# A state-space scan layer with one activation table set in its front, and in its loop a quarter of d*u spread by DMA and multiplied on GpSimd

## The reference, cut to what matters

```
d   = softplus(W_k xc + bias_k)                      # 96 channels
dA  = exp(d * A[k, c, s])
h_t = h_(t-1) * dA_t + (d_t * u_t) * B_t[s]
y_t = sum over s of h_t[s] * C_t[s]                  # and + Dsk * u
```

## Time and profile before

| | us |
|---|---|
| median of 3 runs | 1020.37 |
| lowest, highest | 1018.37, 1024.68 |
| the profiled execution's own time | 1026.5 |
| its span, first to last instruction | 1024.7 |

### The profile page before, as it was taken

The page is one execution under the profiler, slowest core; times in us unless marked ns, Lnnn a source line. Parts: engine busy times, 40 slices in busy tenths (PEclk is TensorE's granted clock), DMA queues, the critical chain, the costliest instruction groups (busy, mean ns, idle before and its releaser), DMA issues. The chain is left out here.

```text
span 1024.7 us, 17912 instructions
## 1 busy us (share of the span) xinstructions
PE 889.6 (87%) x6186; PEld 592.7 (58%) x6186; DVE 748.7 (73%) x1612; ACT 572.8 (56%) x1007; POOL 486.8 (48%) x502
## 2 busy tenths in 40 slices
PE   8769999997699987879988679999999987766985
PEld 3323333334258972234445359899888845566985
DVE  6479999998476537877875776788888685583665
ACT  2765455431246645978963645777776265264762
POOL 0006666663206632799882005377777400034873
PEclk8889999999799987555556979999999987978997
DMA  5067666631300009300000192999995573203464
GB/s 141 1 175 189 156 168 169 167 104 28 65 1 1 2 13 267 3 1 2 1 2 1 47 233 77 260 264 266 258 266 149 159 223 106 62 24 104 167 211 163
DMA packets 73018, 120.19 MB, mean 117 GB/s; under 512 B 24704, under 2 KB 47632, under 8 KB 72928
## 3 DMA queue, kind: packets, MB, share of 16 engines
q1 hardware_dynamic: 68080, 108.85, 40.1%
q0 software_dynamic: 4848, 10.20, 2.9%
HBM read 90.83 MB, written 19.40 MB: 108 GB/s over the span
## 5 line engine op out<-in xcount | busy, mean ns | idle before, releaser
L464 POOL TENSOR_TENSOR hC<-hs,Cb 128x1024 f32<-128x1024 f32 x47 | 110.8, 2357 | 124.9 <-DVE hs L503 124.9
L503 DVE TENSOR_TENSOR_SCAN hs<-ps_l,dBu 128x1024 f32<-128x1024 f32 x48 | 109.9, 2290 | 2.8 <-ACT ps_l L595 1.2
L663 PE MATMUL ps_l<-hC,selT 128*96 128x512 f32 x192 | 93.2, 609 | 1.5 <-POOL hC L464 1.5
L595 ACT ACTIVATE ps_l<-d_sp,Am 128x1020 f32<-128x1020 f32 x48 | 53.5, 1115 | 71.5 <-DVE hs L503 71.3
L648 PE MATMUL ps_l<-du,sel 96*128 96x512 f32 x192 | 90.5, 593 | 1.4 <-DVE dBu L496 1.4
L2192 POOL DMA_INDIRECT scratch_y<-m_o,m_xg x42 | 69.2, 1648 | 9.6 <-issue 9.6
L787 POOL TENSOR_TENSOR n_Pl<-n_PT,n_Ph 128x352 f16<-128x352 f32 x48 | 40.8, 852 | 66.5 <-ACT n_Ph L915 49.0
L2255 DVE TENSOR_TENSOR m_h_lo<-m_h,m_h_hi 128x512 f16<-128x512 f32 x62 | 42.8, 691 | 35.1 <-POOL m_h_hi L2169 32.3
L2831 POOL DMA_INDIRECT scratch_g<-g_U,g_slot x16 | 21.4, 1335 | 98.8 <-DVE g_who L2956 92.2
L2585 PE MATMUL ps_m<-m_wd_hi,m_h_hi 128*128 128x192 f16 x248 | 62.2, 251 | 6.2 <-DVE m_h_lo L2255 4.0
L2169 POOL CAST m_h_hi<-m_h 128x512 f16<-128x512 f32 x50 | 40.5, 810 | 53.7 <-DVE m_h L2244 53.7
(11 more groups left out here) (575 smaller groups left out, 2922.9 us busy)
## 6 DMA issues: line engine op xcount, KB each, us to landing
d_sp<-scan_d SPq DMA_DIRECT2D x48, 512.0 KB, 4.6
m_sta<-in_m_ua SPq DMA_DIRECT2D x25, 512.0 KB, 4.4
m_stb<-in_m_ub SPq DMA_DIRECT2D x50, 256.0 KB, 5.7
m_std<-in_m_dn SPq DMA_DIRECT2D x25, 384.0 KB, 6.8
gw_dn_in<-gw_dn SPq DMA_DIRECT2D x10, 576.0 KB
scratch_x<-zero SPq DMA_DIRECT2D x1, 4416.0 KB, 16.5
m_xg<-scratch_x SPq DMA_DIRECT2D x21, 193.0 KB, 6.6
gw_dn_in<-in_g_dn SPq DMA_DIRECT2D x5, 576.0 KB, 8.6
```

The source lines that it names most:

```text
L464: pool.tensor_tensor(hC[:, n % 2, :], hs[:, n % 2, :], Cb[:, which(n), :], ALU.mult).then_inc(weighted, 1)
L503: v.tensor_tensor_scan(hs[:, n % 2, ::step], dA(n)[:, ::step], dBu[:, n % 2, ::step], 0.0, ALU.mult, ALU.add).then_inc(scanned, 1)
L595: act.activation(dst[:, :, o:o + L - 1], d_sp[:, n % NSP, :].rearrange("p (b t) -> p b t", t=L)[:, :, o:o + L - 1], ACT.Exp, scale=Am[:, c ...
L663: mm = pe.matmul(ps[0:DI, 6 + half, :], selT[:, n % NG, :], hC[:, n % 2, half * BANK:(half + 1) * BANK], start=(n == STEPS), stop=(m == ST ...
```

## The change

1. ScalarE loads one table set by hand ahead of the front. Its stream goes direction by direction: softplus parts, logarithm and copies of B and C interleaved. VectorE's stream follows it (`softplus(i)`, `products(i)`), TensorE multiplies `W` for two directions ahead of the `zb` projection. The last direction's two products move from VectorE to GpSimd.
2. In the loop the last 256 of 1024 columns (`WIDE` = 768 is the rest, `L` = 256) of d*u are stored to DRAM and spread by DMA into `du_sp` (128 KB a step, on SyncE's queue behind each `d_sp`), and GpSimd multiplies them by B (`part`). VectorE multiplies the other 768 in one instruction (`wide`), one step ahead of the scan; TensorE spreads 768 columns instead of 1024.
3. `dBu` and `hC` get a third buffer, and TensorE's `add` runs four steps behind `spread` instead of two.

The core of the diff (semaphores for the last direction, `d_last` and `du_last`, stand for `d_ready` and `du_ready`):

```diff
+        WIDE = T - L
+        BEHIND = 4
+        du_sp = ctx.sb("du_sp", [P, NSP, L])
-        dBu = ctx.sb("dBu", [P, 2, T])
+        dBu = ctx.sb("dBu", [P, 3, T])
-        hC = ctx.sb("hC", [P, 2, T])
+        hC = ctx.sb("hC", [P, 3, T])
...
# SyncE
+                def store_du(i):
...
+                    sync.dma_start(du_dram[ORDER[i]], du[:, i, WIDE:T]).then_inc(stored_du[i], 16)
...
                     sync.dma_start(d_sp[:, n % NSP, :], rows.unsqueeze(0).broadcast_to([NS, CG, T])).then_inc(spread_d[n % NSP], 16)
...
+                    if n >= NSP:
+                        sync.wait_ge(dBu_part, n - NSP + 1)
+                    rows = du_dram[which(n), g * CG:(g + 1) * CG, :]
+                    sync.dma_start(du_sp[:, n % NSP, :], rows.unsqueeze(0).broadcast_to([NS, CG, L])).then_inc(spread_du[n % NSP], 16)
...
# GpSimd
+                def part(n):
...
+                    pool.wait_ge(spread_du[n % NSP], 16 * (n // NSP + 1))
+                    if n >= 3:
+                        pool.wait_ge(scanned, n - 2)
+                    pool.tensor_tensor(dBu[:, n % 3, WIDE:T], du_sp[:, n % NSP, :], Bb[:, which(n), WIDE:T], ALU.mult).then_inc(dBu_part, 1)
+                part(0)
+                part(1)
...
+                pool.tensor_tensor(dd[:, last, :], dd[:, last, :], du[:, last, :], ALU.add).then_inc(d_last, 1)
...
+                pool.tensor_tensor(du[:, last, :], dd[:, last, :], xc[:, ORDER[last] % 2, :], ALU.mult).then_inc(du_last, 1)
                 for n in range(N - 1):
+                    if n >= 1:
+                        part(n + 1)
                     pool.wait_ge(scanned, n + 1)
...
# VectorE
+                def wide(n):
...
+                    v.wait_ge(du_bc, n + 1)
+                    if n >= 3:
+                        v.wait_ge(scanned, n - 2)
+                    v.tensor_tensor(dBu[:, n % 3, 0:WIDE], banks(4, 6)[:, 0:WIDE], Bb[:, which(n), 0:WIDE], ALU.mult).then_inc(dBu_done, 1)
+                wide(0)
+                for n in range(N):
+                    if n + 1 < N:
+                        wide(n + 1)
+                    v.wait_ge(dBu_done, n + 1)
+                    v.wait_ge(dBu_part, n + 1)
                     v.wait_ge(dA_done, n + 1)
...
# ScalarE
+                act.preload_act_table_set("natural_log_exp_and_others")
...
# TensorE
+                    if n >= 1:
+                        pe.wait_ge(dBu_done, n)
+                    for at, end in ((0, BANK), (BANK, WIDE)):
+                        mm = pe.matmul(banks(4, 6)[:, at:end], sel[:, n % NG, :], du[:, n // NG, at:end], start=True, stop=True)
...
-                    if n >= 2:
-                        add(n - 2)
+                    if n >= BEHIND:
+                        add(n - BEHIND)
```

More of the change, by code:

```diff
@@ L254, in scan_layer @@
         stored = [S(f"stored{k}") for k in range(KD)]
+        stored_du = [S(f"stored_du{k}") for k in range(KD)]
         spread_d = [S(f"spread_d{j}") for j in range(NSP)]
+        spread_du = [S(f"spread_du{j}") for j in range(NSP)]
+        dBu_part = S("dBu_part")
+        d_last, du_last = S("d_last"), S("du_last")
         started, dA_done, du_bc, dBu_done, scanned, weighted, y_added, y_out, weighted_last = (
@@ L470, in _, with softplus @@
                 v.reciprocal(qw["rc"][:], qw["sc"][:]).then_inc(q_inverse, 1)
[L471 to L476, removed]
+                def softplus(i):
                     v.wait_ge(soft_act, 3 * i + 3)
@@ L556, in _, with log @@
                     act.activation(ex[:, i % 2, :], ex[:, i % 2, :], ACT.Exp, scale=-1.0).then_inc(soft_act, 1)
[L557 to L563, removed]
+                def log(i):
                     act.wait_ge(soft_vec, 3 * i + 2)
                     act.activation(dd[:, i, :], dd[:, i, :], ACT.Ln).then_inc(logged, 1)
-                for i in range(1, KD):
-                    for j in range(2):
-                        take(i, j)
+                act.preload_act_table_set("natural_log_exp_and_others")
+                act.wait_ge(loaded_p, 64)
+                softplus(0)
+                act.activation(Am[:, :], Alog[:, :], ACT.Exp).then_inc(A_done, 1)
+                act.wait_ge(A_done, 1)
+                act.activation(Am[:, :], Am[:, :], ACT.Copy, scale=-1.0).then_inc(A_done, 1)
+                softplus(1)
+                log(0)
+                softplus(2)
+                take(0, 0)
+                take(0, 1)
+                log(1)
+                softplus(3)
+                take(1, 0)
+                take(1, 1)
+                log(2)
+                take(2, 0)
+                take(2, 1)
+                log(3)
+                take(3, 0)
+                take(3, 1)
                 def integer(w, i):
@@ L643, in spread @@
                     if n % NG == 0:
[L644 to L649 removed]
+                        if n // NG == KD - 1:
+                            pe.wait_ge(du_last, 1)
+                        else:
+                            pe.wait_ge(du_ready, n // NG + 1)
+                    if n >= 1:
+                        pe.wait_ge(dBu_done, n)
+                    for at, end in ((0, BANK), (BANK, WIDE)):
+                        mm = pe.matmul(banks(4, 6)[:, at:end], sel[:, n % NG, :], du[:, n // NG, at:end], start=True, stop=True)
+                    mm.then_inc(du_bc, 1)
                 def direct():
@@ L666, in add @@
                             mm.then_inc(y_added, 1)
-                for n in range(N + 2):
+                for n in range(N + BEHIND):
                     if n < N:
```

106 lines of the change are left out of this document (66 added, 40 removed).

## The result

| | before | changed |
|---|---|---|
| median of 4 runs, us | 1022.53 | 996.46 |
| lowest, highest | 1018.37, 1027.69 | 993.16, 999.74 |
| the profiled execution's span | 1024.7 | 991.0 |
| front, from the first W product to the first scan | 41.41 | 34.7 |
| loop, first scan's start to last scan's end | 166.99 | 148.04 |

The ratio is 0.9723, with a 95% interval of 0.9684 to 0.9763. The layer took 25.1 us less in the trace: the front 6.7 and the loop 19.0 less, with 0.6 more ahead of them. The rest of the program took 8.6 us less in this one execution. In eleven more programs with the same code behind the layer it took 780.9 to 788.7, so the spans of the two profiled executions (33.7 us apart) flatter the change; the medians (26.1 us apart) fit the layer.

The account below looks back on a forecast made before the run. VectorE was taken to bound the loop, with TensorE nearly as full. The profiled 1026.5 us, less 7.2 (front) and 20.4 (loop), plus 1.0 (clock), gave 999.9; the same -26.6 on the median 1020.37 gave 993.8, range 988 to 1006.

Parts of the forecast that it names:

- The likeliest case: Loop: VectorE sets the step at about 3.07 us, giving a total of 988 to 998 us; chance 0.64.
- Step, 3.07 forecast: Loop, VectorE: scan 2.205 plus one 768-column product 0.865 make 3.07 us a step; loop 146.6 instead of 166.99, -20.4 us.
- TensorE, 3.00: fits: Loop, TensorE: narrower spreads cut its work a step from 3.5 to 3.00 us, fitting with 0.07 us to spare.
- GpSimd, 2.357 + 0.637: Loop, GpSimd: hC plus a 256-column product, 2.99 us, 3.05 with two starts; fits with 0.02 us to spare.
- GpSimd becomes the bound: Loop: GpSimd's product takes 0.852 us, making the step 3.21 us; +6.6 us, total 1000; chance 0.13.
- TensorE's clock in the first steps: First four loop steps: without sums TensorE's clock may fall; bounds 0 and 6 us, +1.0 taken.
- DMA, 92% of a limit of 233 GB/s: Loop transfers: 31.4 MB take 135 us of 146.6 at the full queue's rate, so DMA fits.
- The slower rival: Loop: DMA becomes the bound, slower from 1.43 us per 128 KB, 1032 us at 1.7; chance 0.05 including about as before.
- Front, -7.2: Front: loads and waits on ScalarE go, first scan at 65.1 instead of 72.29 us, -7.2; bounds -9.0 and -3.5.
- The overlap of GpSimd and VectorE in the front: Front: VectorE's d*u product beside GpSimd's sum costs nothing, or at most 2.3 us with 1.7 hidden; 0 taken.
- After the loop, nothing: After the last scan: the last hC needs a sum already done and TensorE ends as before; no change.
- The rival that the loop doesn't get shorter through a chain: Loop: a chain of scan, hC, sum, buffer binds the step; only the front's 7.2 us gained, 1013 us; chance 0.03.

Follow-up runs that it names:

- eighth_on_gpsimd: The changed kernel with 128 columns by DMA and GpSimd instead of 256, 896 on VectorE and TensorE; loop 156.6 us, ratio to before 0.9824.
- q288_on_gpsimd: The changed kernel with 288 columns on GpSimd instead of 256, so 736 on VectorE; loop 149.0 us, ratio to before 0.9789.
- warm_start: The changed kernel with eight products of zeros added on TensorE in each of steps 1 to 3; loop 144.8 us, ratio to before 0.9733.
- double_spread: The changed kernel with a second 128 KB spread a step into its own buffer, which GpSimd awaits too; loop 147.4 us, ratio to before 0.9798.
- last_on_vector: The changed kernel with the last direction's two products back on VectorE; front 35.7 us, ratio to before 0.9757.
- no_preload: The changed kernel without the table set loaded; front 43.0 us, ratio to before 0.9862.
- behind_two: The changed kernel with TensorE's sums two steps behind its spreads instead of four; loop 252.1 us, ratio to before 1.0817.

## Why the prediction was right

The forecast was 993.8 in 988 to 1006; the median is 996.46. (The 2.8 us taken off for the lower end are 1.8 of the front and, unsaid there, the 1.0 of the clock.) The likeliest case, VectorE at about 3.07 a step, is the one that came. Against the working, the layer gave 25.1 us of the 26.6:

- **Step, 3.07 forecast.** 3.04 measured. The product of 768 columns takes 0.935, not 0.949, and the scan 2.281 for 2.290. 145.2 of undisturbed loop stand against 146.6.
- **TensorE, 3.00: fits.** It does, with 3.01: 1.72 from the sum to the spread (88.21 - 86.49) and 1.29 from there to the next sum. The factor in the working is wrong (0.857 is six sevenths), but seven eighths of 3.44 are 3.01 as well. eighth_on_gpsimd shows how nearly it fits: with 896 columns TensorE, and not VectorE, sets the step, at 3.22 for 3.18.
- **GpSimd, 2.357 + 0.637.** The product takes 0.724, inside the bounds of 0.57 and 0.852 and above the value taken. But where GpSimd is full each instruction starts 0.04 before its neighbour's end (86.95 + 2.36 = 89.31, next at 89.27; in q288_on_gpsimd on both sides), while I had added 0.06 for two starts: 2.356 + 0.724 - 0.08 = 3.00, 0.04 under VectorE's step. With the product as measured and the starts as I counted them it would have been 3.14 and the bound. Two errors cancelled, and that was luck. The rival "GpSimd becomes the bound" was missed by a hair: q288_on_gpsimd, 32 columns more, is that case.
- **TensorE's clock in the first steps, 1.0 taken of 0 to 6.** 2.9 measured: three waits. warm_start shows the cause. This is the term that was mis-sized most.
- **DMA, 92% of a limit of 233 GB/s.** The margin was wider than said: double_spread moved 265, so no limit lies at 233. 128 KB in 1 KB rows cost no more than about the favourable bound of 0.56. By the share, from the window of the changed kernel over 75 to 200 us (0.94, with 41 steps) to double_spread's (1.06), it is 0.12 x 125 / 41 = 0.37 us each; as no window shown here reads over 1.09, I take this for a lower estimate. An upper one: double_spread moves two of them beside 512 KB in 3.05 us, and if the 512 KB went at its 265 GB/s (1.98 us), 0.53 is left for each. The slower rival, which began at 1.43, was far away.
- **Front, -7.2.** -6.7 by its own length, with luck: in most of the other traces with this front TensorE's clock dips at 53 to 59 us, which the working did not consider, and it is -5.7 (35.7). The last copy of C ends at 61.2 for 60.9 forecast, from a start 0.6 later, and the load is hidden as said. The way from there to the scan took 5.0 (4.2 forecast).
- **The overlap of GpSimd and VectorE in the front, taken at 0.** 0.7 measured. The row that I leaned on, `hC` undisturbed at 2.357 in the loop, has a partner with an operand in PSUM; the front's pair has all its operands in SBUF. There VectorE's product took 3.26 us and GpSimd's two 2.90 and 3.21, for 1.22 (last_on_vector), 2.35 and 2.36 (eighth_on_gpsimd) with nothing beside them, and VectorE's product ended 1.08 us behind GpSimd's sum. My own upper bound, 2.3 less the 1.7 that is hidden, is 0.6 and was the better value.
- **After the loop, nothing.** Nearly: from the last scan's end to VectorE's `ysum` it is 217.09 - 214.20 = 2.9 us, before 1.9. The 1.0 us stand in the rest of the program and are lost in its 8 us of spread.
- **The rival that the loop doesn't get shorter through a chain** was argued away with scan, `hC`, `part`, scan at 5.3 for 6.1 us. That chain was not the dangerous one. The one through TensorE's sums is, and with them two steps behind it makes the loop 85 us longer than before. What saves the change is the edit that my working gave no number, `BEHIND = 4`.

Size for size, against the forecast: -1.42 for the loop's steps, +1.88 for the clock, +0.50 for the front and +0.57 ahead of it make 1.5 us, the difference between 26.6 and 25.1. The medians differ by 26.1.

## What to carry to other kernels

When a wide step is cut evenly among three engines, look at the distance between producer and consumer first: the same change, front included, gains 2.6 to 2.8% with the sums three or four steps behind and loses 8.2% with two. Count the engine that gets the new work at its own width, since GpSimd's 256 columns cost 31% of its 1024 and not 25%. And count the table loads before functions are interleaved: with one set for the whole stage the front took 34.7 us with one load of 1.28; without it (no_preload) there were seven, and at 43.0 the new order gave back all that it had won in the front.

## What the runs showed of the hardware

- TensorE's granted clock fell to 0.50 at the loop's start (windows of the changed kernel from 69 to 76 us), where three spreads in a row waited 0.48, 1.49 and 1.05 us, and in behind_two (105 to 107 us) behind a wait of 2.67 us. After a single wait of 1.64 us in the front it dipped in seven traces of nine and not in those of the changed kernel and q288_on_gpsimd. With eight small products with zeros in the gaps of the loop's start it read 1.00 there (warm_start).
- Products of f32 on GpSimd took 0.457 us for 128 columns, 0.724 for 256, 0.800 for 288 and 2.356 for 1024.
- The same queue reads 233 GB/s of repeated 4 KB rows at a share of 1.04, and 265 GB/s at 1.06 with 1 KB rows among them: a share of about 1 does not say that no more would fit. Landing took 9.8 us there and 5.2 in the changed kernel.
- GpSimd's product of 256 columns took 1.66 us in the changed kernel's front beside VectorE products with both operands in SBUF, and one of these 1.63 instead of 1.22; in the loop, beside VectorE instructions with an operand in PSUM, GpSimd's took 0.724 in the mean, its `hC` 2.35 to 2.37 as before the change, and VectorE's product of 768 columns 0.93 to 0.96.
